# Reordering the hand-over from attention tiles to expert steps: last output product ahead of logits, slots ahead of inner values, GpSimd additions held back

## Chip, cores and metric

One core of one Trainium2 chip. The metric is device microseconds of one execution of the kernel; the median of 3 runs of the kernel before is 1112.19 us (1111.52 to 1112.27).

## What is computed

Input `x` is 4 x 1024 tokens of width 256, all arithmetic in float32. Two layers follow each other, each with a residual:

```
x = x + attention(layernorm(x))     # Nystroem attention, 16 heads, 64 landmarks, 13-tap convolution over tokens, output product with w_fc
x = x + experts(layernorm(x))       # 8 experts, each token goes to 2 of them
```

The attention ends in `out @ w_fc + b_fc`; the kernel adds bias and residual and has the rows `x1` of 128 tokens. The expert layer normalizes `x1`, takes 8 logits per token (`x @ router_w.T`), chooses the two best experts with a jitter threshold and a softmax weight each, and adds for each chosen expert

```
weight * ((silu(x @ w_gate.T) * (x @ w_up.T)) @ w_down.T)
```

## The kernel before, in words

The kernel is written engine by engine, with semaphores between them. There are 36 token steps (`QT`), nine per batch of 1024 tokens; each makes attention scores, exponentials, the weighing by GpSimd, the convolution (`c2_conv`) and, for a tile `m` of 128 tokens, the output product `c2_y(m)`, 16 matmul records into bank 6 of PSUM. Tiles 0 to 31 exist (`MT` is 32). Bank 6 holds one tile at a time, so the next product waits until VectorE has added the residual in `rows_out(m)` (line 1110); TensorE's wait is `bank6_read`.

Tiles are routed in nine groups: seven of four tiles (0 to 6), then group 7 (tiles 28 and 29) and group 8 (tiles 30 and 31). The constants are `LATE` = 6, `NG - 2` = 7, `NG - 1` = 8. The chain for one group is:

- VectorE: `statistics` (lines 1115 and 1116) for each tile, then `inverse_deviations` (1123 to 1131), whose end releases `c2_rs`.
- ScalarE: `norm_rows` (776), one activation for each tile.
- TensorE: `c2_tp`, four transpose records for two tiles (1742). ScalarE: `norm_columns` (783). TensorE: `c2_late_lg`, the logits of two tiles (1758).
- VectorE: `choices` (1146, then 1164 to 1176), whose end releases `d_hot`. TensorE: `c2_counts` (1800). ScalarE: `gap_exponentials` (806).
- VectorE: `slots` (1183 to 1202): weights of the two experts, the counts copied out of PSUM by `take_counts` (1152), places by running sums, and the row indices `idx`, whose end releases `d_meta`.
- GpSimd: `scatter` (587), two indirect DMAs for each tile, which write normalized rows into `xs_d`, sorted by expert.

When group 8 is placed, VectorE counts (`sizes`) and builds tables of work items: `whole_items` (1254 to 1259) and `table` (1263 to 1273). The first table releases `d_units`, on which SyncE loads the sorted rows of the first full items (473), after the scatters have landed.

The expert stage is a chain of 128-token steps `n`, in items `a` of one or two steps. TensorE transposes the rows of an item (`x_columns`, 1846), makes `hidden(0, n)` and `hidden(1, n)` (gate and up products, 1883) and later `down(n)` (1926). ScalarE copies the transposed rows (`rows_transposed`, 813) and takes Silu of the gate product (`gate_out`, 820). VectorE multiplies (`hidden_out`, 1288, which releases `m_hid`) and weighs the result of down (`rows_weighed`, 1300). GpSimd adds the rows to the output (`add_rows`, 608), again an indirect DMA. VectorE also copies each item's gate and up weights (`expert_weights`, 1317). Steps 0 to 4 (items 0 to 2) are "early": their rows belong to an expert chosen after group 4, and were scattered and loaded before. Step 5 is `BLOCK[FIRST]`, the first step of item 3.

Each engine runs its queue in order. What matters around the change is the order written out by hand where the two stages meet. On TensorE, after token step 37:

```
c2_tp(7,0) | late_lg(7,0) x_columns(0) c2_y(31) | hidden(0,0) hidden(1,0) counts(7) c2_tp(8,0)
hidden(0,1) [wait counts of 7 taken] late_lg(8,0) hidden(1,1) down(0) x_columns(1) counts(8) down(1)
hidden(0,2) hidden(1,2) hidden(0,3) x_columns(2) down(2) hidden(1,3) hidden(0,4) down(3) x_columns(3) hidden(1,4) ...
```

The wait in brackets stands because the logits of group 8 and the counts of group 7 lie in the same bank 5. On VectorE the generic `token_step` goes on to step 39: `rows_out(29)` statistics, `inverse_deviations(7)`, `slots(6)`; `rows_out(30)` statistics, `choices(7)`; `rows_out(31)` statistics, `inverse_deviations(8)`; then `hidden_out(0)`, `slots(7)`, `choices(8)`, `hidden_out(1)`, `slots(8)`, `sizes`, `rows_weighed(0)`, the first table, `hidden_out(2)`.

ScalarE has one set of function tables loaded at a time. Exp and Silu are in different sets; the other activations here (Copy, Identity) run under either. The loads are records of their own (ACT_TABLE_LOAD).

## Time and profile before

| | us |
|---|---|
| median of 3 runs | 1112.19 |
| the profiled execution | 1118.69 |
| span in its trace | 1117.0 |
| TensorE busy in the span | 1068.3 |
| VectorE busy | 643.6 |
| ScalarE busy | 319.1 |
| GpSimd busy | 299.3 |

The profiled execution stands 6.50 us above the median. The granted clock of TensorE over its span is 0.995 of full speed. Times in the text are us from the start of the span. The place where the change works lies between 715 and 785 us.

### The profile page before, as it was taken

To read this page: it belongs to the slowest core of one execution; us is meant where nothing else is said; L and a number is where in the kernel's file an instruction comes from. 1 tells how busy PE (TensorE), PEld (TensorE's weight loads), DVE (VectorE), ACT (ScalarE), POOL (GpSimd) and SP (SyncE) were. 2 spreads that over 40 slices of the span, in tenths; PEclk is the share of its full clock that TensorE was granted. 3 is DMA by queue.
4 is the path that set the end of the run, shared out by engine and by line. 5 is a ranking of instruction groups with operands and counts; after the bars stand their busy time and mean duration, and the time that the engine had idled before them with its cause. 6 is when DMAs were issued, how large, how long until landed. Compare 5 with 4: busy or idle time off the path is not lost. (4 is left out here: it accounts for less than half of the span.)

```text
span 1117.0 us, 22941 instructions
## 1 busy us (share of the span) xinstructions
PE 1068.3 (96%) x9126; PEld 857.3 (77%) x9126; DVE 643.6 (58%) x1376; ACT 319.1 (29%) x471; POOL 299.3 (27%) x303
## 2 busy tenths in 40 slices
PE   4999999999989999999999999979999999999996
PEld 4888888888878756666676666768877877878795
DVE  7457755565558576677777778755434434343332
ACT  4433232222324422332332332331122122121210
POOL 6000000000020013225535535551333333423333
PEclk9999999999999999999999999999999999999999
DMA  9300000000300040222411323343423223333122
GB/s 336 125 1 1 1 1 1 1 1 1 97 3 0 2 190 20 105 67 67 144 62 63 104 75 113 109 123 88 87 47 48 47 44 53 49 51 45 20 30 24
DMA packets 48252, 68.27 MB, mean 61 GB/s; under 512 B 8224, under 2 KB 41504, under 8 KB 47136
## 3 DMA queue, kind: packets, MB, share of 16 engines
q1 hardware_dynamic: 34288, 46.83, 13.4%
q0 software_dynamic: 13440, 16.93, 9.1%
q10 hardware_dynamic: 432, 3.24, 0.7%
q8 instruction: 62, 1.02, 0.4%
q14 instruction: 30, 0.25, 0.1%
HBM read 41.43 MB, written 26.59 MB: 61 GB/s over the span
## 5 line engine op out<-in xcount | busy, mean ns | idle before, releaser
L1883 PE MATMUL ps<-mem 128*128 128x256 f32 (+1 forms) x1152 | 221.9, 345 | 0.0
L1883 PEld LDWEIGHTS ps<-mem 128*128 128x128 f32 x1152 | 190.1, 191 | 27.2 <-issue 7.5
L608 POOL DMA_INDIRECT out<-mem x60 | 100.6, 1676 | 196.8 <-DVE mem L1300 151.1
L1288 DVE TENSOR_TENSOR mem<-mem,ps 128x512 f32<-128x512 f32 x66 | 45.3, 687 | 156.8 <-PE ps L1883 131.3
L1729 PE MATMUL ps<-mem 128*128 128x512 f32 x288 | 129.4, 593 | 0.0
L573 POOL TENSOR_TENSOR mem<-mem,small 128x1024 f32<-128x1024 f32 x36 | 68.6, 1906 | 224.8 <-DVE small L1222 120.2
L1926 PE MATMUL ps<-mem 128*128 x480 | 115.3, 384 | 6.6 <-DVE mem L1288 6.6
L820 ACT ACTIVATE mem<-ps 128x512 f32<-128x512 f32 x66 | 39.4, 597 | 285.8 <-PE ps L1883 248.7
L1782 PE MATMUL ps<-mem 128*128 128x256 f32 x512 | 119.4, 387 | 0.0
L1479 PE MATMUL ps<-mem 128*128 128x256 f32 x512 | 117.3, 382 | 0.6 <-ACT mem L694 0.6
L1440 PE MATMUL ps<-mem 128*128 128x256 f32 x512 | 114.5, 380 | 0.0
L1782 PEld LDWEIGHTS ps<-mem 128*128 128x128 f32 x512 | 95.5, 192 | 15.0 <-issue 3.2
L1440 PEld LDWEIGHTS ps<-mem 128*128 128x128 f32 x512 | 95.6, 190 | 12.7 <-issue 0.3
L1479 PEld LDWEIGHTS ps<-mem 128*128 128x128 f32 x512 | 94.8, 190 | 13.5 <-issue 0.8
L1926 PEld LDWEIGHTS ps<-mem 128*128 128x128 f32 x480 | 89.4, 192 | 18.1 <-issue 7.3
L1729 PEld LDWEIGHTS ps<-mem 128*128 128x128 f32 x288 | 54.2, 190 | 54.8 <-issue 52.7
L587 POOL DMA_INDIRECT xs_d<-mem,idx x64 | 62.4, 975 | 56.5 <-DVE idx L1202 40.6
L1774 PEld LDWEIGHTS ps<-mem 128*64 128x64 f32 x1152 | 57.1, 137 | 20.7 <-issue 20.3
L1774 PE MATMUL ps<-mem 128*64 128x116 f32 x1152 | 65.1, 266 | 0.8 <-POOL mem L573 0.8
L795 ACT ACTIVATE mem<-ps 128x928 f32<-128x928 f32 (+2 forms) x36 | 31.6, 877 | 119.8 <-PE ps L1774 89.7
L1317 DVE COPY mem<-mem 128x2048 f32 x51 | 62.1, 1238 | 5.7 <-issue 2.9
L1300 DVE TENSOR_SCALAR mem<-ps,mem 128x256 f32<-128x256 f32 x66 | 29.7, 480 | 48.4 <-PE ps L1926 46.4
(239 smaller groups left out, 1383.7 us busy)
## 6 DMA issues: line engine op xcount, KB each, us to landing
mem<-w_gu SPq DMA_DIRECT2D x9, 1024.0 KB, 5.8
mem<-xs_d SPq DMA_DIRECT2D x22, 260.0 KB, 2.8
mem<-x SPq DMA_DIRECT2D x8, 512.0 KB, 8.8
mem<-x SPq DMA_DIRECT2D x32, 128.0 KB, 2.3
out<-mem SPq DMA_DIRECT2D x32, 128.0 KB, 1.7
mem<-w_down SPq DMA_DIRECT2D x8, 512.0 KB
xnt_d<-mem ACTq DMA_DIRECT2D x3, 1056.0 KB, 5.6
mem<-xnt_d SPq DMA_DIRECT2D x3, 1056.0 KB, 4.8
```

Of the source, the lines that this page charges most:

```text
L573: pool.tensor_tensor(a1[:, u], ex[:, u].rearrange("p (h c) -> p h c", h=H), ri[:, 16 * u:16 * u + 16].unsqueeze(2).to_broadcast([P, H, M]) ...
L587: pool.indirect_dma_start(out=xs_d, out_offset=bass.IndirectOffsetOnAxis(ap=idx[:, u, v, c:c + 1].bitcast(U32), axis=0), in_=xd[:, u, v, c ...
L608: pool.indirect_dma_start(out=out_rows, out_offset=bass.IndirectOffsetOnAxis(ap=rows_to.bitcast(U32), axis=0), in_=ys[:, r % YRING], in_of ...
L1288: dve.tensor_tensor(hid[:, n % 2], sil[:, n % 2], bank(2 + n % 2), ALU.mult).then_inc(s("m_hid"), 1)
L1317: dve.tensor_copy(v, w_gu_s[:, e]).then_inc(s("m_w"), 1)
L1440: mm = pe.matmul(bank(t // 2)[:, t % 2 * 2 * P:(t % 2 + 1) * 2 * P], xnts[b][:, k, HALO + P * t:HALO + P * t + P], g3c[:, b, k, j * P:(j + ...
L1479: mm = pe.matmul(bank(6)[:, k * 2 * P:(k + 1) * 2 * P], xna[:, b, t, k * P:(k + 1) * P], e3s[m % 4][:, t], start=(t == 0), stop=(t == RT - 1))
L1729: mm = pe.matmul(bank(2 * u + half), xnt2[b % 2][:, k, TO * t:TO * t + P], g1c[:, b, k, 512 * half:512 * half + 512], start=(k == 0), stop ...
L1774: mm = pe.matmul(bank(4, 2)[c:c + 64, (h // 2) * P:(h // 2) * P + TO], a1[:, q % 2, h], band[:, h], start=True, stop=True)
L1782: mm = pe.matmul(bank(6)[:, 0:D], cvt[:, j, at_:at_ + P], pm[:, b, j], start=(j == 0), stop=(j == J - 1))
L1883: mm = pe.matmul(bank(2 * c + n % 2)[:, i * size:(i + 1) * size], w[:, k, c, f * P:(f + 1) * P], xst[:, a % 2, k, 0:size], start=(k == 0), ...
L1926: mm = pe.matmul(bank(down_bank(a, b))[:, 0:D], hid[:, u, i * size + b * P:i * size + (b + 1) * P], w_d_s[:, e, f], start=(f == 0), stop=( ...
```

## The change

It leaves every computation as it is and changes the order of instructions on four engines, with one added wait.

```
@@ gpsimd
             for u in range(X1):
                 pool.wait_ge(s(f"x1_out{u}"), 16 * (MT // X1))
+            pool.wait_ge(s("m_hid"), 3)
             for r in range(EBLK):
                 wait_alone(pool, "m_y", r + 1)
                 add_rows(r, xs_e[:, r, D + 1:D + 2])
@@ scalar
             norm_columns(NG - 2, 0)
             rows_transposed(0)
-            gap_exponentials(NG - 2)
-            gate_out(0)
             norm_rows(NG - 1, 0)
             norm_rows(NG - 1, 1)
+            gate_out(0)
             norm_columns(NG - 1, 0)
+            gap_exponentials(NG - 2)
             gate_out(1)
             gap_exponentials(NG - 1)
@@ vector: slots(g) is now slot_weights(g), up to take_counts(g), and slot_places(g), the rest
-            for i in range(QT + 4):
+            for i in range(QT + 1):
                 token_step(i)
+            rows_out(MT - 3)
+            statistics(MT - 3, NG - 2)
+            inverse_deviations(NG - 2)
+            slot_weights(LATE)
+            rows_out(MT - 2)
+            slot_places(LATE)
+            statistics(MT - 2, NG - 1)
+            rows_out(MT - 1)
+            statistics(MT - 1, NG - 1)
+            inverse_deviations(NG - 1)
+            choices(NG - 2)
             dve.wait_ge(s("c2_a1"), QT)
+            slots(NG - 2)
             hidden_out(0)
-            slots(NG - 2)
             choices(NG - 1)
             hidden_out(1)
             slots(NG - 1)
             sizes()
             rows_weighed(0)
             whole_items(0, 8)
+            hidden_out(2)
             table(2 * P, u_eid, u_row, "d_units")
-            hidden_out(2)
@@
                     table(P, t_eid, t_row, "d_rest")
-                if n == BLOCK[FIRST] + 1:
+                if n == BLOCK[FIRST] + 2:
                     taken(NT, P)
                     whole_items(C - 1, 5)
                     table(C, c_eid, c_row, "d_rest")
@@ tensor
             c2_tp(NG - 2, 0)
             pe.wait_ge(s("c2_cvt"), cvt_count(QT - 1))
+            bank6_read(last)
+            c2_y(MT - 1)
             c2_late_lg(NG - 2, 0)
             x_columns(0)
-            bank6_read(last)
-            c2_y(MT - 1)
             pe.wait_ge(s("e_w_in"), 16)
             pe.wait_ge(s("c2_sub"), QT)
             hidden(0, 0)
             hidden(1, 0)
-            c2_counts(NG - 2)
             c2_tp(NG - 1, 0)
             pe.wait_ge(s("d_taken"), NG - 2)
             hidden(0, 1)
+            c2_counts(NG - 2)
             pe.wait_ge(s("d_taken"), NG - 1)
             c2_late_lg(NG - 1, 0)
             hidden(1, 1)
```

## Rows read from the trace of the kernel before

**Rows 1.** Page, busy us of each engine, share of the span, instructions.

```profile
PE 1068.3 (96%) x9126; PEld 857.3 (77%) x9126; DVE 643.6 (58%) x1376; ACT 319.1 (29%) x471; POOL 299.3 (27%) x303
```

**Rows 2.** Timeline of TensorE: start, us, engine, line, operation, count, [idle before it <-releaser].

```profile
720.48 0.66 PE L1742 MATMUL ps<-ids,mem 128*128 128x128 f32 x4 [0.42 <-ACT mem L776]
721.91 1.24 PE L1758 MATMUL ps<-rw,mem 128*128 128x8 f32 x8 [0.78 <-ACT mem L783]
...
723.89 4.67 PE L1782 MATMUL ps<-mem 128*128 128x256 f32 x16
728.39 3.62 PE L1883 MATMUL ps<-mem 128*128 128x256 f32 x16
...
733.93 0.66 PE L1742 MATMUL ps<-ids,mem 128*128 128x128 f32 x4 [1.57 <-ACT mem L776]
...
743.38 5.34 PE L1883 MATMUL ps<-mem 128*128 128x256 f32 x24
748.56 0.38 PE L1846 MATMUL ps<-ids,mem 128*128 128x128 f32 x2
753.76 3.44 PE L1926 MATMUL ps<-mem 128*128 x8 [4.82 <-DVE mem L1288]
...
783.68 1.99 PE L1926 MATMUL ps<-mem 128*128 x8 [0.88 <-DVE mem L1288]
```

**Rows 3.** Busy time by stretch: length, PE, PEld, DVE, ACT, POOL, PEclk, DMA share, GB/s.

```profile
719.20:722.60 3.40, 2.20 (x15) 1.54 (x14) 3.02 (x19) 1.82 (x3) 0.00 (x0) 1.00 0.00 0
722.60:726.00 3.40, 3.40 (x13) 2.98 (x13) 2.78 (x16) 0.60 (x1) 2.56 (x3) 0.50 0.33 116
...
732.80:736.20 3.40, 2.27 (x12) 1.83 (x12) 1.62 (x8) 1.67 (x3) 0.00 (x0) 1.00 0.74 296
```

**Rows 4.** Timeline of ScalarE, same columns.

```profile
732.36 1.52 ACT L776 ACTIVATE mem<-mem,small 128x512 f32<-128x512 f32 x2 [0.33 <-issue]
...
736.97 1.28 ACT L806 ACT_TABLE_LOAD   x1
740.41 0.23 ACT L806 ACTIVATE mem<-mem 128x32 f32<-128x32 f32 x1 [2.16 <-DVE mem L1176]
...
748.50 0.60 ACT L820 ACTIVATE mem<-ps 128x512 f32<-128x512 f32 x1 [5.20 <-remote]
```

**Rows 5.** Timeline of GpSimd, same columns.

```profile
751.11 1.58 POOL L608 DMA_INDIRECT out<-mem  x1 [0.30 <-issue]
```

**Rows 6.** Timeline of VectorE, same columns.

```profile
719.96 0.22 DVE L1152 COPY mem<-ps 128x64 f32<-128x64 f32 x1
...
722.01 0.43 DVE L1110 TENSOR_TENSOR mem<-ps,mem 128x256 f32<-128x256 f32 x1
...
728.59 0.42 DVE L1110 TENSOR_TENSOR mem<-ps,mem 128x256 f32<-128x256 f32 x1 [2.47 <-PE ps L1782]
...
732.16 0.16 DVE L1131 SCALAR_TENSOR_TENSOR small<-small 128x2 f32<-128x2 f32 x1
...
735.04 0.18 DVE L1183 TENSOR_TENSOR mem<-mem 128x32 f32<-128x32 f32 x1
...
737.30 0.17 DVE L1202 CAST idx<-mem 128x4 int32<-128x4 f32 x1
...
740.20 0.17 DVE L1176 TENSOR_TENSOR mem<-mem 128x16 f32<-128x16 f32 x1
...
752.91 0.69 DVE L1288 TENSOR_TENSOR mem<-mem,ps 128x512 f32<-128x512 f32 x1 [2.65 <-remote]
...
776.16 0.16 DVE L1278 TENSOR_SCALAR small<-small 128x8 f32<-128x8 f32 x1
...
780.18 0.24 DVE L1273 TENSOR_SCALAR tab<-tab,small 128x24 int32<-128x24 f32 x1
```

**Rows 7.** Timeline of SyncE's DMA issues, same columns.

```profile
751.31 3.83 SPq L473 DMA_DIRECT2D mem<-xs_d  x4
```

**Rows 8.** Page, DMA issues: count, KB each, median us from issue to landing.

```profile
mem<-xs_d SPq DMA_DIRECT2D x22, 260.0 KB, 2.8
```

More of the change, by code:

```diff
@@ L614, in _ @@
                 pool.wait_ge(s(f"x1_out{u}"), 16 * (MT // X1))
+            pool.wait_ge(s("m_hid"), 3)
             for r in range(EBLK):
@@ L855, in _ @@
             rows_transposed(0)
-            gap_exponentials(NG - 2)
-            gate_out(0)
             norm_rows(NG - 1, 0)
             norm_rows(NG - 1, 1)
+            gate_out(0)
             norm_columns(NG - 1, 0)
+            gap_exponentials(NG - 2)
             gate_out(1)
@@ L1178, in slots, with slot_weights @@
             def slots(g):
+                slot_weights(g)
+                slot_places(g)
+            def slot_weights(g):
                 (m, n), (u, v0) = GROUPS[g], HOME[g]
@@ L1195, in slots, with slot_places @@
                     take_counts(g)
+            def slot_places(g):
+                n, (u, v0) = GROUPS[g][1], HOME[g]
+                t = both[:, :, 0:n]
                 dve.wait_ge(s("d_taken"), g + 1)
@@ L1342, in token_step @@
                     choices(g)
-            for i in range(QT + 4):
+            for i in range(QT + 1):
                 token_step(i)
+            rows_out(MT - 3)
+            statistics(MT - 3, NG - 2)
+            inverse_deviations(NG - 2)
+            slot_weights(LATE)
+            rows_out(MT - 2)
+            slot_places(LATE)
+            statistics(MT - 2, NG - 1)
+            rows_out(MT - 1)
+            statistics(MT - 1, NG - 1)
+            inverse_deviations(NG - 1)
+            choices(NG - 2)
             dve.wait_ge(s("c2_a1"), QT)
+            slots(NG - 2)
             hidden_out(0)
-            slots(NG - 2)
             choices(NG - 1)
@@ L1354, in _ @@
             whole_items(0, 8)
+            hidden_out(2)
             table(2 * P, u_eid, u_row, "d_units")
-            hidden_out(2)
             dve.wait_ge(s("wgu_in"), 16 * E)
@@ L1375, in _ @@
                     table(P, t_eid, t_row, "d_rest")
-                if n == BLOCK[FIRST] + 1:
+                if n == BLOCK[FIRST] + 2:
                     taken(NT, P)
@@ L1934, in _ @@
             pe.wait_ge(s("c2_cvt"), cvt_count(QT - 1))
+            bank6_read(last)
+            c2_y(MT - 1)
             c2_late_lg(NG - 2, 0)
             x_columns(0)
-            bank6_read(last)
-            c2_y(MT - 1)
             pe.wait_ge(s("e_w_in"), 16)
@@ L1942, in _ @@
             hidden(1, 0)
-            c2_counts(NG - 2)
             c2_tp(NG - 1, 0)
@@ L1946, in _ @@
             hidden(0, 1)
+            c2_counts(NG - 2)
             pe.wait_ge(s("d_taken"), NG - 1)
```

## The prediction

> **What bounds the kernel now.** I read the page first: TensorE is busy 96% of the span and no other engine passes 58% [rows 1]. So an edit is worth what it takes out of TensorE's queue, idle time or time at the lower clock, and only where nothing behind it takes it back. TensorE's timeline between the stages comes next [rows 2]. It has four waits: 0.42 us, 0.78 us, 1.57 us and 4.82 us. Two groups of products ran at half pace as well. The output product of tile 31 took 4.67 us where the 16 records of the same shape behind it took 3.62, and `down(2)` took 3.44 us for 8 records where 1.73 is usual (8 x 0.216: 24 such records start and pass in the 5.18 us from 743.38 to 748.56). The busy time by stretch shows why: from 722.6 the granted clock is 0.50, that is 1.2 GHz in place of 2.4, and ahead of that TensorE had waits, transposes and products of 8 columns; in 732.8 to 736.2, behind 1.57 us of idle, it stayed at 1.00 [rows 3]. Then comes the full expert stage, with one wait of 0.88 us at 783.68 [rows 2].
>
> The long wait deserves a second look. `down(2)` waits for `hidden_out(2)` at 752.91, and that engine's own wait, 2.65 us, has the releaser "remote", no instruction of this trace [rows 6]. The same holds for ScalarE at 748.50: it reads the first of three products that TensorE issued from 743.38, done by 0.216 x 8 at about 745.1, and starts 3.4 us after that [rows 2, 4]. VectorE and ScalarE get on some 0.2 us after GpSimd's second addition ends at 752.69 [rows 5, 6]. So TensorE's signals came late here, for a reason that the trace doesn't name. The wait and the lower clock behind it cost 4.82 + 1.71 = 6.53 us. The profiled execution, 1118.69, stands 6.50 us over the median of 1112.19. I take it from this that the ordinary runs lack this stall. Without it VectorE would be at 743.8 behind its count of rows (740.4 + 0.6 for `hidden_out(1)` + 2.4 for the slots + 0.4), weigh two blocks in 0.9 and make the first table in 3.6 (the third took 4.26 with 0.7 of `taken` ahead, 776.16 to 780.42 [rows 6]): 748.3. `hidden_out(2)` would end at 749.0, as TensorE gets to `down(2)` at 748.95.
>
> **The change, part by part.** I follow the new order in the profiled execution's time.
>
> Bank 6. VectorE now has `rows_out(30)` ahead of the places of group 6. The weights with the counts' copy end at 720.18 [rows 6], so it runs at 720.2 in place of 722.01 and ends at 720.63. TensorE's transposes of group 7 stay at 720.48 and take 0.44 us to the next start; `c2_y(31)` then starts at 720.9, in place of 723.89, and needs 3.45 us to the next start at full clock: 724.4. The wait of 0.78 us vanishes, since the copy that it was for now runs beside the product. The logits of group 7 take 0.9 and `x_columns(0)` 0.44: 725.75. Here a new wait appears. ScalarE's copy of these columns (0.60, as the activation of the same size [rows 4]) was hidden by `c2_y(31)` and now isn't: hidden(0,0) starts at 726.6, idle 0.85 us. Both hidden products end at 730.05, where before they did at 731.85 (728.39 + 3.45) [rows 2]. That is 1.8 us gained, 1.05 of it the lower clock.
>
> Group 8's normalization. `rows_out(31)` is ready at 724.6. From 728.59 to the end of the deviations at 732.32 was 3.73 us [rows 6]: 728.35 now. `norm_rows` stands ahead of `gate_out(0)`, takes 1.52 [rows 4], ends at 729.9, and TensorE is busy to 730.05. So the 1.57 us wait is gone. Transposes 0.45 and hidden(0,1) 1.73 end at 732.2, counts(7) at 732.55; `choices(7)` (2.9 us, from 737.47 to 740.37 in group 8 [rows 6]) had ended near 731.0.
>
> The wait ahead of group 8's logits. It is for `take_counts(7)`, now behind `choices(7)` and behind the exponentials of group 7, and VectorE waits for these. On ScalarE these stood ahead of `gate_out(0)`, under the same tables as the exponentials before. Now they stand between two Silus, so there are two loads of tables more. ScalarE: load 729.9 to 731.2, Silu to 731.8, `norm_columns` to 732.4, load to 733.7, exponentials (0.23) to 733.9. Slot weights take 1.26 us to the end of the counts' copy (their share of 2.4): 735.2. TensorE stands idle from 732.55 to 735.2, 2.65 us, with `hidden_out(0)`, `choices(8)` and all of VectorE's queue behind the same wait. A load costs 1.28 us by its own record [rows 4]. What it holds up can't be less; the nearest activation behind one starts 3.44 us after the load's start (736.97 to 740.41), but that one waited for VectorE [rows 4]. I take 1.28, and keep 3.44 as the upper end.
>
> The Trainium skill, page "ScalarE: Activation LUTs", section "What ACT_TABLE_LOAD costs", puts a switch of tables at about 2.66 us, the load of 1283 ns and a drain of 1380 ns. The load agrees with the trace; the drain no row shows. By that price the wait of TensorE would be 2.8 us longer.
>
> On to `down(2)`. Logits of group 8 0.9 and hidden(1,1) 1.75 end at 737.85. Before it was 739.04 (733.93 + 0.49 + 1.90 + 0.91 + 1.81). **Lead 1.2 us.** Then down(0), x_columns(1), counts(8), down(1) as before: `hidden_out(0)` comes at 737.0, the choices of group 8 end at 739.8, `hidden_out(1)` at 740.4, when TensorE gets there, and the third load of tables lies beside `down(0)`. The three hidden products and x_columns(2) end at 747.55. `slots(8)` runs 740.4 to 742.8 (2.4, from 735.04 to 737.47 [rows 6]), sizes and weighing to 744.1, item counts (1.3 of the 3.6) to 745.4, `hidden_out(2)` with the up product at 745.8, done at 746.5, since it is ahead of the table (2.3 us). So `down(2)` doesn't wait.
>
> GpSimd. Its second addition starts at 751.11, the first 1.9 us ahead of it (1.58 and 0.30 of issue [rows 5]), right behind the scatters. These move by the 0.5 us of group 8's indices, so they last to about 748.7, after `m_hid` has reached 3. The added wait costs nothing; the cover is the scatter, and if `hidden_out(2)` were late the additions would move by as much, ahead of buffers that are free for 8 rows. The scatter of group 6 moves 0.45 us later, behind it nothing waits.
>
> The first table ends at 748.7. Group 8's indices come at 742.8, before at 743.3; its scatters and SyncE's row loads, which wait for their landing, move by the same 0.5 us: 750.8 for 751.31, landed 2.8 us later at 753.6 [rows 7, 8]. `x_columns(3)` comes at 754.5. It holds by 0.9 us: this is what is late next.
>
> The third table moves from step 6 to step 7. It ended at 780.42 and pushed a weight copy, a weighing and `hidden_out(7)` behind it, for which TensorE stood 0.88 us [rows 2, 6]. Now `hidden_out(7)` comes first, and the 4.2 us of table lie before the next product is done. **Gain 0.9 us.** SyncE gets the entry for the quarter items some 5 us later, and the first of them is wanted 20 us later.
>
> Sum: 1.2 + 0.9 = 2.1 us against ordinary runs, 1112.19 - 2.1 = 1110.1. Against the profiled execution 6.5 + 2.1 = 8.6: 1118.69 - 8.6 = 1110.1, provided that its own signals come in time.
>
> **The rivals.** *The lower clock moves on.* TensorE has 3.9 us with little but a wait and narrow products (732.2 to 736.1). The stretch of 719.2 to 722.6 led to a fall, the one with 1.57 us idle didn't [rows 3], and this lies between them and longer. A fall like that of 753.76 costs 1.7 us: 1111.8. *The loads of tables cost more* (slower). If each of the two on the path costs 2.66 us, within the 3.44 bound, that is 2.76 us more, the wait is 5.4 us, like the 4.82 us behind which the clock fell: 1110.1 + 2.8 + 1.7 = 1114.6. With the fall, the change loses time from 0.2 us more for each load, and by over 0.2% from 1.3. For it speaks that no row shows an activation right behind a load; against it that the loads themselves start without a gap. *The stall is in ordinary runs too.* Then the gain is 6.5 + 1.2 + 0.9 = 8.6, 1103.6, or 2 us less if the signal for `hidden_out(2)`, sent at 745.8, still comes 3.4 us late like the one at 748.50: 1105.6. Against it stands the match of 6.53 and 6.50. *The lead is given back*, at the landing of rows or at a signal that comes late before 735: no change, 1112.2.
>
> **How the numbers follow.** Forecast 0.40 (own range 1109 to 1111), clock 0.20, loads 0.13, stall 0.17, given back 0.10. A measurement tells 0.2%, 2.2 us, from no change, so the forecast lies on that bound and I put 0.22 of its 0.40 on the faster side: with 0.17 of the stall and 0.03 of the clock case, 0.42. Slower is the loads' case with a little of the others: 0.15. Same 0.43. The range takes in the clock case and the near end of the stall and goes up to most of the loads': 1105.2 to 1113.8.
>
> **What would show it.** In the changed profile: `c2_y(31)` near 720.9 in 3.7 us; a wait of about 2.7 us before the second L1758 group, released by VectorE's L1152; five ACT_TABLE_LOADs between 726 and 745 for three; no wait at `down(2)`; none near 775 to 785. A span near 1108.4, where the clock stays whole. I am wrong if that wait is over 4 us, if the clock drops behind it, or if the time falls by more than 5 us, which would put the stall into the ordinary runs.

## The result, and the profile after

| | before | after |
|---|---|---|
| median, 14 runs each, taken beside each other | 1112.01 us | 1114.07 us |
| lowest to highest | 1110.94 to 1113.80 | 1112.63 to 1115.68 |
| profiled execution | 1118.69 | 1115.68 |
| its span | 1117.0 | 1114.0 |

The ratio is 1.0017, interval 1.001 to 1.0024: some 2 us slower, where 2.1 us faster was forecast, and outside the range. The profiled execution before, with its long stall, lies outside the 14 timed runs, so the two profiles stand the other way round than the medians do. Each is compared with the prediction's sum, not with the other.

TensorE after, same columns as [rows 2]. L1801 is now `c2_y`, L1761 `c2_tp`, L1777 the late logits, L1902 `hidden`, L1945 `down`.

```profile
719.79 0.66 PE L1761 MATMUL ps<-ids,mem 128*128 128x128 f32 x4 [0.43 <-ACT mem L777]
720.28 3.62 PE L1801 MATMUL ps<-mem 128*128 128x256 f32 x16
...
725.96 3.69 PE L1902 MATMUL ps<-mem 128*128 128x256 f32 x16 [0.78 <-ACT mem L814]
729.49 0.60 PE L1761 MATMUL ps<-ids,mem 128*128 128x128 f32 x4
...
737.25 1.88 PE L1777 MATMUL ps<-rw,mem 128*128 128x8 f32 x8 [5.08 <-DVE mem L1153]
738.98 3.76 PE L1902 MATMUL ps<-mem 128*128 128x256 f32 x8
742.53 2.97 PE L1945 MATMUL ps<-mem 128*128 x8
...
753.35 1.89 PE L1945 MATMUL ps<-mem 128*128 x8
```

Up to 732 it goes as predicted. The output product runs right behind the transposes at full clock (3.62 us for the 4.67 of [rows 2]), the new wait for the copied columns is 0.78 us (forecast 0.85), and group 8's transposes wait no more (1.57 before). Then comes a wait of 5.08 us where 2.65 was forecast, and behind it the logits and hidden(1,1) take twice their time, and `down(0)` takes 2.97 us where the next ones take 1.97. `down(2)` at 753.35 has no wait; before, it had 4.82 us.

Busy time by stretch of after, same columns as [rows 3]: the granted clock falls from 1.00 to 0.50, which is 1.2 GHz for 2.4, behind a stretch in which TensorE has no instruction at all.

```profile
732.80:736.20 3.40, 0.00 (x0) 0.00 (x0) 0.19 (x1) 2.42 (x4) 0.00 (x0) 0.75 0.11 39
736.20:739.60 3.40, 2.35 (x10) 2.26 (x11) 2.89 (x17) 2.85 (x3) 0.38 (x1) 0.50 0.00 0
```

ScalarE after, as [rows 4]. L784 is `norm_columns`, L807 the exponentials, L821 Silu.

```profile
729.04 1.28 ACT L821 ACT_TABLE_LOAD   x1
730.33 0.60 ACT L821 ACTIVATE mem<-ps 128x512 f32<-128x512 f32 x1
733.74 0.60 ACT L784 ACTIVATE mem<-ps 128x512 f32<-128x512 f32 x1 [2.81 <-remote]
734.35 1.28 ACT L807 ACT_TABLE_LOAD   x1
735.64 0.23 ACT L807 ACTIVATE mem<-mem 128x32 f32<-128x32 f32 x1
735.89 1.28 ACT L821 ACT_TABLE_LOAD   x1
737.18 0.60 ACT L821 ACTIVATE mem<-ps 128x512 f32<-128x512 f32 x1
```

Here is the difference. The transposes were issued from 729.49, and hidden(0,1) behind them starts at 729.93, so the columns of group 8 stand in PSUM near 730.1. ScalarE is free at 730.93. It copies them at 733.74, and the releaser is "remote": the signal is late. The load of tables, the exponentials, VectorE's slot weights (first at 735.97) and the copy of the counts stand behind. The loads themselves cost what was forecast: 734.35 plus 1.28 is 735.63, and the activation starts at 735.64.

GpSimd after, as [rows 5]: the first and the eighth of group 6's scatters, and the first addition.

```profile
722.36 1.01 POOL L587 DMA_INDIRECT xs_d<-mem,idx  x1 [9.25 <-DVE idx L1210]
...
731.25 0.96 POOL L587 DMA_INDIRECT xs_d<-mem,idx  x1 [0.30 <-issue]
...
753.61 1.62 POOL L608 DMA_INDIRECT out<-mem  x1 [0.30 <-issue]
```

The addition follows group 8's scatters after 0.30 us of issue, so the added wait on `m_hid` costs nothing. The eighth scatter ends at 732.21, and the late copy starts 1.53 us after it. The experiments turn on that distance.

VectorE after, as [rows 6]: `hidden_out(2)` waits 1.38 us for the up product that it multiplies, and TensorE gets to `down(2)` behind it.

```profile
751.77 0.69 DVE L1296 TENSOR_TENSOR mem<-mem,ps 128x512 f32<-128x512 f32 x1 [1.38 <-PE ps L1902]
```

The chain of all of TensorE's waits from 715 to the end, after (waiting line, releaser: us in total, times, longest). The wait near 783 of [rows 2] is gone; the 0.9 left stands at the end of the kernel.

```profile
PE ps L1777 <- DVE mem L1153: 5.1, 1, 5.1
PE ps L1945 <- DVE mem L1296: 0.9, 1, 0.9
PE ps L1819 <- DVE mem L1111: 0.8, 1, 0.8
PE ps L1902 <- ACT mem L814: 0.8, 1, 0.8
PE ps L1761 <- ACT mem L777: 0.4, 1, 0.4
```

### The profile page after: what moved, and what is told of

The parts are those of the page before. It is cut to its first block, busy times and chain, and to the rows that moved or that the text cites. A ratio compares the mean times of both kernels' runs of the same rounds, so it can differ in the third digit from the quotient of the medians.

```text
span 1114.0 us, 22943 instructions
## 1 busy us (share of the span) xinstructions
PE 1067.5 (96%) x9126; PEld 857.1 (77%) x9126; DVE 642.8 (58%) x1376; ACT 321.5 (29%) x473; POOL 300.1 (27%) x303
## 3 DMA queue, kind: packets, MB, share of 16 engines
q10 hardware_dynamic: 432, 3.24, 0.7%
## 4 chain that ended last, share of the span: by engine, by line
PE 83%; DVE 6%; issue 4%; POOL 3%; DMA 2%; ACT 2%; another core or an unknown queue 0%; POOLq 0%; DVEq 0%; ACTq 0%
PE ps L1902 17%; PE ps L1498 10%; PE ps L1459 9%; PE ps L1801 9%; PE ps L1945 9%; PE ps L1748 8%; PE ps L1793 5%; PE ps L1886 2%; DMA out<-mem 2%; PE ps L1615 1%; PE ps L1865 1%; PE ps L1433 1%; PE ps L1634 1%; PE ps L1939 1%; PE ps L1513 1%
## 5 line engine op out<-in xcount | busy, mean ns | idle before, releaser
L1902 PE MATMUL ps<-mem 128*128 128x256 f32 (+1 forms) x1152 | 223.7, 347 | 0.8 <-ACT mem L814 0.8
L1902 PEld LDWEIGHTS ps<-mem 128*128 128x128 f32 x1152 | 191.1, 192 | 28.6 <-issue 8.5
L1801 PE MATMUL ps<-mem 128*128 128x256 f32 x512 | 118.4, 384 | 0.0
L821 ACT ACTIVATE mem<-ps 128x512 f32<-128x512 f32 x66 | 39.4, 597 | 273.3 <-PE ps L1902 245.2
L1945 PE MATMUL ps<-mem 128*128 x480 | 114.7, 382 | 0.9 <-DVE mem L1296 0.9
L1801 PEld LDWEIGHTS ps<-mem 128*128 128x128 f32 x512 | 94.7, 190 | 14.7 <-issue 3.2
L1945 PEld LDWEIGHTS ps<-mem 128*128 128x128 f32 x480 | 89.2, 192 | 12.0 <-issue 1.1
```

Of the source, the lines that this page charges most:

```text
L1801: mm = pe.matmul(bank(6)[:, 0:D], cvt[:, j, at_:at_ + P], pm[:, b, j], start=(j == 0), stop=(j == J - 1))
L1902: mm = pe.matmul(bank(2 * c + n % 2)[:, i * size:(i + 1) * size], w[:, k, c, f * P:(f + 1) * P], xst[:, a % 2, k, 0:size], start=(k == 0), ...
L1945: mm = pe.matmul(bank(down_bank(a, b))[:, 0:D], hid[:, u, i * size + b * P:i * size + (b + 1) * P], w_d_s[:, e, f], start=(f == 0), stop=( ...
```

## The experiments

The kernels were timed in five groups, each on one chip beside runs of the kernel before, and every ratio is to those. "Below" and "above" compare medians; a ratio with its interval is worked out from the single runs, so it can differ a little from the ratio of the medians. The chips differ, as it turned out, and this is part of the answer.

### First chip: parts of the change, and the kernel before (1109.79 us, 27 runs)

**before_again**, the kernel before, one execution with its profile.

> The kernel before, profiled once more, to see whether the 4.82 us wait at the down product of step 2 (753.76 in the first profile) belongs to the kernel or to that one execution. Theory S (the stall belongs to single executions): the wait is under 1 us here, the down product runs at full clock, and the profiled time is within 2 us of the median of 1112.0. Rival (it is in every execution): a wait of 4 to 5 us again, and the profiled time as near to the median as it can be with that wait in both.

Measured 1109.04 us, span 1107.3. The stall of the first profile is absent; `down(2)` starts without a wait:

```profile
745.63 1.99 PE L1926 MATMUL ps<-mem 128*128 x8
```

So the 6.5 us of stall are no fixed part of the kernel, as assumed. But 1109 is also 3 us below the median of 1112: "without the stall" and "an ordinary run on the first chip" are not the same thing.

**exp_first**: the exponentials of group 7 ahead of both Silus, so two loads of tables fewer.

```
             norm_rows(NG - 1, 1)
+            gap_exponentials(NG - 2)
             gate_out(0)
             norm_columns(NG - 1, 0)
-            gap_exponentials(NG - 2)
             gate_out(1)
```

> The changed kernel, with the exponentials of group 7 on ScalarE put ahead of the Silu of step 0, so that the two additional loads of tables are gone; all else as changed. Theory L (the loads and the Silu, the copy of columns and their signal in front of the exponentials make TensorE wait 5.08 us ahead of the logits of group 8, and the clock falls behind it): that wait is under 1.5 us, the clock stays whole there, and the time is 3.5 to 5.5 us under the changed kernel, 1108.6 to 1110.6, ratio to before 0.997 to 0.9985. Rival E (the late wait for the exponentials is not what costs in ordinary runs; the earlier output product or the held back additions do): within 1 us of the changed kernel, ratio 1.001 to 1.0025.

Measured 1107.85, ratio 0.9982 (0.9973 to 0.9991). TensorE's timeline:

```profile
733.51 1.03 PE L1777 MATMUL ps<-rw,mem 128*128 128x8 f32 x8 [0.88 <-ACT mem L784]
734.39 3.48 PE L1902 MATMUL ps<-mem 128*128 128x256 f32 x8
```

The wait is 0.88 us and its releaser the copy of columns. The clock fell behind it all the same. The copy of columns (L784) starts at 732.77, as ScalarE comes free. That is 0.07 us behind GpSimd's eighth scatter, so this row alone can't tell whether the signal was in time; the other rows of this chip show that it was ("What the runs say together"). The kernel after wasn't run here, so what the exponentials' place is worth by itself is open.

**table3_later**: the kernel before with only the third table moved.

```
-                if n == BLOCK[FIRST] + 1:
+                if n == BLOCK[FIRST] + 2:
```

> The kernel before with only the third table moved from step 6 to step 7. Theory (the prediction's term): the wait of 0.88 us at the down product of step 7 goes, nothing comes back, 0.9 us faster, ratio 0.9992. Rival: the later row loads of the quarter items or the delayed table make TensorE wait elsewhere, ratio 1.000 or above.

Measured 1108.65, ratio 0.9992 (0.9981 to 1.0002). In the chain of waits `down` waits once for 0.9 us, where before_again has 1.8 in two:

```profile
PE ps L1926 <- DVE mem L1288: 0.9, 1, 0.9
```

**tail_only**: this and the two other late parts, without the new order at the front.

```
+            pool.wait_ge(s("m_hid"), 3)
...
+            hidden_out(2)
             table(2 * P, u_eid, u_row, "d_units")
-            hidden_out(2)
```

> The kernel before with the three parts of the change that lie behind the hand-over: the GpSimd additions behind m_hid 3, the inner values of step 2 ahead of the first table, the third table one step later. Theory L: none of these loses time, ratio 0.997 to 0.9995 (0.9 us for the third table, and up to 2 us more if the inner values of step 2 were late in ordinary runs too). Rival G (one of these three is what made the change slower): ratio 1.001 or more.

Measured 1109.14, ratio 0.9984 (0.9975 to 0.9993), so the tail is a gain of 0.8 to 2.8 us on this chip by the interval, 0.65 by the medians, though its one profile had the lower clock in the output product of tile 31, as [rows 2] has.

### Second chip: the wait ahead of group 8's logits (before 1118.10 us, 33 runs)

**after_again**, the kernel after.

> The changed kernel once more, beside the others on the same chip. Its first profile had a wait of 5.08 us ahead of the logits of group 8, of which 2.81 us was ScalarE waiting for a late signal of the transposes ahead. Theory L (the two loads lie on the path in every execution, the late signal only in some): the wait is 2.4 to 3.2 us, the clock falls or stays, ratio to before 1.0005 to 1.002. Rival D (the late signal is all of it): the wait is 2.3 us too, but the time is under before, ratio 0.998 to 0.9995, as the prediction had it.

Measured 1115.27, ratio 0.9982 (0.9967 to 0.9997). The same change that loses 2 us in the first measurement gains 2 to 3 here, because the kernel before takes 1118.1 (1112.68 to 1119.96), close to the 1118.69 of its profile with the stall. These 33 times fall into two groups with nothing between them: nine from 1112.68 to 1114.83 (middle 1113.81) and 24 from 1117.07 to 1119.96 (middle 1118.4). Against the lower group the kernel after is 1.5 us slower here too. The wait is there as in after: 5.30 us, with ScalarE idle for 3.02 us ahead of the copy of columns, releaser "remote".

**silu0_copy**: it leaves out the Silu of step 0 and copies the gate product instead.

```
-                act.activation(sil[:, n % 2], bank(n % 2), ACT.Silu)
+                act.activation(sil[:, n % 2], bank(n % 2), ACT.Copy if n == 0 else ACT.Silu)
```

> The changed kernel with the Silu of step 0 replaced by a plain copy, so that step 0 takes the gate product without its Silu; the order stays, the exponentials of group 7 stay behind it, but the two loads of tables ahead of them are gone. Theory L (loads): the wait ahead of the logits of group 8 falls by 2.5 us to under 0.7 us, and the time falls by 2.5 to 4.5 us under the changed kernel. Rival O (the late place of the exponentials behind the Silu and the copy of columns costs, not the loads): the wait stays over 2 us.

Measured 1113.50, ratio 0.9966 (0.9951 to 0.9981). ScalarE and TensorE:

```profile
733.54 0.60 ACT L784 ACTIVATE mem<-ps 128x512 f32<-128x512 f32 x1 [4.41 <-remote]
734.03 0.22 ACT L807 ACTIVATE mem<-mem 128x32 f32<-128x32 f32 x1
```

```profile
735.63 1.88 PE L1777 MATMUL ps<-rw,mem 128*128 128x8 f32 x8 [3.83 <-DVE mem L1153]
```

Two loads fewer took 1.5 us off the wait (5.30 to 3.83), one load and not two. ScalarE's own wait shows why: it grew from 3.02 to 4.41. The first load lay beside the late signal and was free; only the second stood behind it. And 3.83 us remain with neither load, so the loads are not the cause of what the forecast missed.

**exp_columns_first**: exponentials and columns ahead of both Silus.

```
             norm_rows(NG - 1, 1)
-            gate_out(0)
-            norm_columns(NG - 1, 0)
             gap_exponentials(NG - 2)
+            norm_columns(NG - 1, 0)
+            gate_out(0)
             gate_out(1)
```

> The changed kernel with the exponentials of group 7 and then the copy of group 8's columns ahead of the Silu of step 0. With the exponentials alone moved, TensorE waited 0.88 us for that copy, which stood behind a load and a Silu. Theory L: the wait is 0.2 to 0.5 us, ratio to before 0.997 to 0.9985, by up to 1 us better than with the exponentials alone. Rival: the Silu of step 0 is now late for the inner values, TensorE waits at the first down product, ratio 0.9985 or above.

Measured 1111.49, ratio 0.9947 (0.9928 to 0.9965), 3.8 us below the kernel after.

```profile
736.49 0.60 ACT L784 ACTIVATE mem<-ps 128x512 f32<-128x512 f32 x1 [3.47 <-remote]
```

The signal is as late as ever, but nothing is left behind it: TensorE waits 2.55 us, for the copy itself. This profile is of the slowest of its ten executions (1115.45); the second and third profile of this order, at 1110.82 and 1111.28, show the same wait as 2.30 and 2.42.

**front_only**: the kernel after without its three late parts.

> The changed kernel without its three later parts: no wait of GpSimd for m_hid, inner values of step 2 behind the first table, third table at step 6. Theory L (the hand-over's own order loses what the later parts win): 1 to 1.6 us slower than the changed kernel beside it, ratio to before 1.001 to 1.003. Rival G: the same as the changed kernel within 0.5 us.

Measured 1116.13, ratio 0.9997 (0.9981 to 1.0012), 0.86 us above the kernel after. In the chain of waits the wait near 783 is back:

```profile
PE ps L1944 <- DVE mem L1295: 1.8, 2, 0.9
```

### Third chip: what makes the signal late (before 1113.22 us, 27 runs)

**after_third**, the kernel after.

> The changed kernel as the reference of this group. Two chips differed: on one the kernel before ran in 1109.8 us and no signal of TensorE was late in five profiles of four kernels, on the other it ran in 1118.1 and signals were late by 2 to 6 us while the last weight load and GpSimd's scatters ran. Theory (late signals are a matter of the chip, and the change trades one place of harm for another): where the profile shows no late signal at the copy of columns of group 8, the wait ahead of its logits is 2.3 to 2.9 us and the ratio to before 0.998 to 1.0005; where it shows one, the wait is about 5.2 us, and the ratio is set by whether the kernel before has its own stall at the down product of step 2 in most of its runs (0.997 to 0.999) or not (1.001 to 1.003).

Measured 1114.85, ratio 1.0017 (1.0008 to 1.0026), the wait 5.12 us, ScalarE idle for 2.83 us ahead of the copy. (The expectation speaks of five profiles on the first chip; there are four, of four kernels.)

**load_late**: the last load of expert weights, which lands in this stretch, is held back.

```
                         sp.wait_ge(s("c2_y"), m + 1)
+                        if m == MT - 1:
+                            sp.wait_ge(s("m_hid"), 2)
```

> The changed kernel, with the last 1 MB load of gate and up weights (issued at 724.8) held back on SyncE until the inner values of step 1 are made, near 743. It is wanted near 755. Theory W (this load is what makes TensorE's signals late at 729 to 734): no wait of ScalarE with the releaser remote at the copy of columns, the wait ahead of the logits falls from about 5.2 to about 2.5 us, the time falls by 2 to 4 us. Rival S (GpSimd's scatters do it): the signal is as late as in the reference.

Measured 1115.01, ratio 1.0015 (1.0006 to 1.0024). The load is issued at 743.59 and the signal is late as before:

```profile
733.71 0.60 ACT L786 ACTIVATE mem<-ps 128x512 f32<-128x512 f32 x1 [2.81 <-remote]
```

This theory fell.

**scatter_late**: all eight scatters of group 6 wait until group 8's columns are copied.

```
                         if sent_at(g, h) == i and 2 * h < GROUPS[g][1]:
+                            if g == LATE and h == 0:
+                                pool.wait_ge(s("c2_x1t"), PAIRS[NG])
                             scatter(g, 2 * h)
```

> The changed kernel, with the eight scatters of group 6 (from 722.4) held back on GpSimd until the columns of group 8 are copied, near 731 to 734. Rival S (GpSimd's scatters make TensorE's signals late): no remote wait at the copy of columns, the wait falls to about 2.5 us. Theory W (the weight load does): the signal stays late, the wait stays over 4 us. If either alone removes it, both together are needed for the lateness.

Measured 1117.96, ratio 1.0047 (1.0033 to 1.006), 3 us worse than after. At the old place all is in time:

```profile
733.76 1.16 PE L1779 MATMUL ps<-rw,mem 128*128 128x8 f32 x8 [2.17 <-DVE mem L1155]
```

That is the forecast's wait of 2.65 us, with both loads on its path. The clock fell behind it all the same: hidden(1,1), next in line, takes 3.55 us where 1.97 is usual. But group 6's and 7's scatters are now one run of twelve, ending at 746.71, and the next signal is late by far more (ScalarE):

```profile
747.37 0.60 ACT L816 ACTIVATE mem<-ps 128x512 f32<-128x512 f32 x1 [8.75 <-remote]
```

**exp_columns_second**, the order of exp_columns_first on this chip.

> The changed kernel with the exponentials of group 7 and the copy of group 8's columns ahead of the Silu of step 0, a second time. Theory L: 3 to 4.5 us under the changed kernel on this chip too (1111.5 against 1115.3 the first time). Rival: under 1 us, the first difference was one of that chip.

Measured 1111.52, ratio 0.9986 (0.9977 to 0.9995), 3.3 us below after_third.

### Fourth chip: cutting the run of scatters (before 1112.36 us, 27 runs)

**after_fourth**, the kernel after.

> The kernel after, for comparison on this chip. If the run of scatters holds TensorE's signals: the copy of group 8's columns starts 1.5 to 1.8 us after the eighth scatter of group 6 ends, the wait ahead of the logits is 5.1 to 5.3 us. If this is a chip without late signals: the copy starts behind the Silu without a releaser 'remote', the wait is near 2.2 to 2.7 us, and the time is 1 us or more below the kernel before.

Measured 1114.19, ratio 1.0015 (1.0006 to 1.0024); GpSimd's eighth scatter, and ScalarE's copy 1.49 us after its end:

```profile
731.03 0.96 POOL L587 DMA_INDIRECT xs_d<-mem,idx  x1 [0.30 <-issue]
```

```profile
733.48 0.60 ACT L784 ACTIVATE mem<-ps 128x512 f32<-128x512 f32 x1 [2.78 <-remote]
```

**scatter_split**: as scatter_late, with `h == 1` for `h == 0`, so that four go at once and four wait.

> The last four of group 6's eight scatters wait until group 8's columns are copied, so that the first run of four ends near 727.3. Theory (a run of scatters holds the signals until it has ended): the columns are copied near 730.3 with no releaser 'remote', the wait ahead of the logits is 2.2 to 2.7 us, and the copy does not follow the fourth scatter by 1.5 us. The four moved ones run from 731 to 736, and signals sent in them may be late, the next in need being those for down(0) and the logits of group 8. If nothing else is late, 3 to 4 us below after_fourth; if the lateness moves on, as with scatter_late, between 2 below and 1 above. Rival (the lateness belongs to the place or to a transfer there, not to the scatters): the copy of columns still starts near 733.7 and the wait is still 5.1, time as after_fourth. On a chip without late signals both are equal within 0.1%.

Measured 1111.73, ratio 0.9993 (0.9984 to 1.0002), 2.5 us below after_fourth. The copy of columns starts at 731.36 behind the Silu, the wait is 2.17 us, and the clock is still whole for the logits (1.06 us for the 1.88 of after), but not for hidden(1,1) behind them:

```profile
734.87 1.06 PE L1779 MATMUL ps<-rw,mem 128*128 128x8 f32 x8 [2.17 <-DVE mem L1155]
735.78 3.45 PE L1904 MATMUL ps<-mem 128*128 128x256 f32 x8
```

The four held scatters and group 7's four follow each other now, a new run of eight that ends at 742.69, and 1.60 us after that:

```profile
741.73 0.96 POOL L587 DMA_INDIRECT xs_d<-mem,idx  x1 [0.30 <-issue]
```

```profile
744.29 0.60 ACT L816 ACTIVATE mem<-ps 128x512 f32<-128x512 f32 x1 [4.60 <-remote]
```

**exp_columns_split**: the same split on top of exp_columns_first.

> As scatter_split, with the exponentials of group 7 and the copy of group 8's columns ahead of both Silus. Theory: no late signal at the copy of columns, so no wait over 1 us ahead of the logits, where the same order without the split showed 2.3 to 2.6 us; 4 to 6 us below after_fourth, if nothing behind is late. Rival (place or transfer): the wait stays 2.3 to 2.6 us and the time 3.3 to 3.8 us below after_fourth.

Measured 1111.52, ratio 0.9994 (0.9985 to 1.0004), 2.7 us below after_fourth and under the 4 expected. The wait ahead of the logits is 0.28 us, and behind it the clock stays whole (hidden(1,1) 1.97 us). The run of eight behind it ends at 741.22, the signal comes at 742.81, and the three hidden products wait for it:

```profile
743.46 7.11 PE L1904 MATMUL ps<-mem 128*128 128x256 f32 x24 [3.94 <-ACT mem L816]
```

### Fifth chip: pauses between the runs (before 1117.51 us, 29 runs)

**exp_columns_third**, the order of exp_columns_first.

> The exponentials and columns ahead of the Silus, group 6's eight scatters in one run, for comparison on this chip. On a chip with late signals: copy of group 8's columns 1.5 to 1.8 us after the eighth scatter, wait 2.3 to 2.6 us ahead of the logits.

Measured 1111.14, ratio 0.9952 (0.9937 to 0.9968), the wait 2.42 us.

**two_pauses** and **three_pauses**: on top of it, group 7's scatters wait for group 8's counts, and in the second kernel group 8's for the third Silu.

```
+                            if g == LATE and h == 1:
+                                pool.wait_ge(s("c2_x1t"), PAIRS[NG])
+                            if g == NG - 2:
+                                pool.wait_ge(s("d_taken"), NG)
+                            if g == NG - 1:                  # three_pauses alone
+                                pool.wait_ge(s("m_sil"), 3)
```

> As exp_columns_third, with group 6's last four scatters held until group 8's columns are copied, and group 7's four until the counts of group 8 are taken; group 7's and group 8's follow each other, a run of eight from about 739. Theory (the length of a run decides): no copy with releaser 'remote' before 740, wait ahead of the logits under 0.5 us, VectorE's copy of the counts of group 8 near 737.5 instead of 742.9; a late signal 1.5 us after the end of the last run, near 750, which may hold hidden_out(2) and down(2): between 2 and 5 us below exp_columns_third where this costs nothing, equal where it costs 3. Rival (each scatter behind the first four delays signals, pause or not): a 'remote' copy between 733 and 740, and no gain on exp_columns_third.

> As two_pauses, with group 8's four scatters held as well, until the gate product of step 2 is through Silu, so that all of the runs have four. Theory: no releaser 'remote' on ScalarE or VectorE between 725 and 752, the wait at down(2) under 0.5 us, 3 to 6 us below exp_columns_third, or less where group 8's rows then land too late for x_columns(3). Rival: a 'remote' copy remains and the time is that of exp_columns_third or above.

Measured 1113.82 and 1114.08, ratios 0.9976 (0.9959 to 0.9993) and 0.9983 (0.9967 to 1.0): both 2.7 to 2.9 us worse than the order without pauses. The first half is as the theory has it: no late signal before 740, a wait of 0.28 us. But with the indices of group 8 ready earlier, its four scatters and the two additions join group 7's, ten in one run. VectorE's `hidden_out(3)` and TensorE's `down(3)` in two_pauses:

```profile
755.29 0.69 DVE L1300 TENSOR_TENSOR mem<-mem,ps 128x512 f32<-128x512 f32 x1 [5.26 <-remote]
```

```profile
756.13 3.51 PE L1949 MATMUL ps<-mem 128*128 x8 [4.30 <-DVE mem L1300]
```

That is the stall of the kernel before, one step later: 5.26 for its 2.65 at VectorE, 4.30 for 4.82 at TensorE, the lower clock behind it [rows 2, 6]. `down(2)` itself, at 746.37, had no wait. The third pause did nothing: the Silu it waits for had ended at 742.32 and group 7's scatters lasted to 744.4. So a run of four was not tried there.

### What the runs say together

The last scatter or addition of a run, and the first late start on another engine behind its end:

| kernel | length of the run | ends | late start | distance |
|---|---|---|---|---|
| after | 8 | 732.21 | 733.74 | 1.53 |
| after_again | 8 | 732.53 | 734.26 | 1.73 |
| after_fourth | 8 | 731.99 | 733.48 | 1.49 |
| exp_columns_first | 8 | 734.72 | 736.49 | 1.77 |
| scatter_split | 8, later | 742.69 | 744.29 | 1.60 |
| exp_columns_split | 8, later | 741.22 | 742.81 | 1.59 |
| scatter_late | 12 | 746.71 | 747.37 | 0.66 |
| before, group 6 | 8 | 732.70 | 734.44 | 1.74 |
| before [rows 5, 6] | 4, a gap of 1.09, 6 | 752.69 | 752.91 | 0.22 |
| two_pauses | 10 | 755.22 | 755.29 | 0.07 |
| three_pauses | 10 | 754.04 | 754.11 | 0.07 |

The lateness follows the scatters, not a place in the program: moving the run moves it. The profiles not in the table (silu0_copy, front_only, after_third, load_late, exp_columns_second and exp_columns_third) have the same run of eight and distances of 1.51 to 1.72. The distance is no rule, though. The table takes starts behind the end of a run, and there are late ones inside runs as well: 745.60 and 748.50 in the kernel before, 749.35 in two_pauses, 748.20 and 749.65 in three_pauses.

Nor does the length of a run decide. In the attention stage GpSimd issues four scatters at a time, and ScalarE's copy of the convolution's product starts late behind them; in the kernel before, the fourth ended at 709.83 and the product was made at 709.1:

```profile
710.91 0.94 ACT L795 ACTIVATE mem<-ps 128x928 f32<-128x928 f32 x1 [3.72 <-remote]
```

In after, the copy at 596.77 comes 3.0 us after its product and 0.86 us after a run of four. TensorE doesn't wait for these. Other runs of four to six held nothing up, as the one of six from 748.54 in after, so what makes one run harmful and another not is open.

On the first chip none of this is seen. Its four profiles have no start with the releaser "remote" on ScalarE or VectorE in the whole trace; each of the other sixteen, the two first profiles included, has at least three ahead of 713 alone. The load on the DMA engines doesn't make the difference here: from 730 to 732 they are as busy in before_again (1.04, 411 GB/s) as in after from 728 to 730 (1.00, 390). In table3_later the run of eight ends at 731.99, and the copy of group 8's columns starts at 731.97, 0.75 us behind the start of the transposes that release it:

```profile
731.97 0.60 ACT L783 ACTIVATE mem<-ps 128x512 f32<-128x512 f32 x1 [0.75 <-PE ps L1742]
```

What sits between the scatters and a signal of TensorE, whether GpSimd's issuing or the transfers that it issues, and why one chip lacks it, stays open.

The clock is a second thing. In every profile of the new order with a wait of 0.88 us or more ahead of group 8's logits it fell to 0.50 at the logits or right behind them, with the signal in time (scatter_late, scatter_split) or not. Only with the wait at 0.28 us did it hold. From group 8's transposes to `down(0)` the forecast has 7.80 us and after 13.04; with the signal in time it is 9.26 in scatter_late and 9.00 in scatter_split. So the late signal costs about 4 us of the difference, and the clock 1.2 to 1.5 us net even without it.

## Why the prediction was wrong

**The step that failed** is the term "2.65 us, idle from 732.55 to 735.2", together with the sentence that the sum holds "provided that its own signals come in time". They don't. And the sum's other condition, "where the clock stays whole", fails by itself: behind a wait of 2.17 us with the signal in time, shorter than the forecast one, hidden(1,1) still took 3.24 and 3.39 us to the next start for 1.75 (scatter_split, scatter_late). Set against the profile, the sum closes. The wait began at 732.17, 0.38 earlier than forecast (this execution was 0.69 us ahead at the transposes of group 7 already), and took 2.43 us more than 2.65. The clock fell behind it, so that the logits took 1.73 us to the next start for 0.9, and hidden(1,1) 3.55 for 1.75: 2.63 more. `down(0)` begins at 742.53 instead of 737.85, 4.68 late. From there to `down(2)` it is 10.82 us for 9.91 in [rows 2], 0.91 more, by `down(0)` at the lower clock. Together 5.59 us (against the sum; the text's own place for `down(2)`, 747.55, is 0.2 us earlier than its sum has it), and the span of 1114.0 is 5.6 above the forecast's 1108.4. Nothing outside this stretch is missing. The medians differ by less, 1114.07 - 1110.1 = 3.97; the profiled execution is the slowest of the 14, and how the others saved 1.6 us wasn't seen. after_again and after_fourth, with 2.16 and 2.41 us for `down(0)` in place of 2.97, point to the clock.

The mechanism stood in the text with a wrong price. It was found in [rows 4, 6] as "TensorE's signals came late here", and carried as one clause of the last rival, "a signal that comes late before 735", with no change as its worst. It was taken as an accident of one execution at one place, where it belongs to a kind of work, GpSimd's scatters, and eight of them stand beside this very step in every execution. The rows to see it were at hand: seen beside GpSimd's timeline, the two late starts of [rows 4, 6] stand in and right behind one run of scatters and additions. The 0.2 us between GpSimd's last addition and VectorE's start was noted and not followed up. And behind the run of eight itself the trace of before has a late start, `hidden_out(0)`, 1.74 us after the eighth scatter:

```profile
734.44 0.69 DVE L1288 TENSOR_TENSOR mem<-mem,ps 128x512 f32<-128x512 f32 x1 [2.12 <-remote]
```

`slots(7)` stands behind it, so group 7's scatters start at 738.28 and end 1.09 us ahead of group 8's; in before_again `hidden_out(0)` starts at 729.38 and that gap is 2.77 us. So the long stall of the kernel before may follow from this earlier late signal. No run tests that.

**Other steps.** Bank 6 and the earlier output product: right, to 0.2 us in each part. The GpSimd wait that costs nothing: right. `down(2)` without a wait: right, and as forecast VectorE is there before the up product (751.77). What the forecast left out is that the signals must come in time there too. They did; group 7's and 8's scatters stand 4.57 us apart, where before they had 1.09. That the gap did it is argued from two_pauses, which closed it and brought a stall back. The third table, forecast 0.9: its wait is gone in both orders, and the runs give 1.1 us (table3_later, by the medians; its interval just takes in no change) and, for the tail as a whole, 0.86 (front_only against after) and 0.65 (tail_only).

**The rivals.** *Loads that cost 2.66 each* was the slower one, and its time, 1114.6, is near the result, by luck: its mechanism is refuted. Three activations start 1.29 us after their load started. The page "ScalarE: Activation LUTs" of the Trainium skill, section "What ACT_TABLE_LOAD costs", adds a drain of 1380 ns to a load; no record here shows it. silu0_copy took two loads away and 3.83 us of wait were left. *The lower clock moves on*: it did, in all of the profiles of after, and in exp_first behind only 0.88 us of idle. This rival was right in its mechanism: its 1.7 us is near the 1.5 to 1.6 that hidden(1,1) lost with the signal in time, and half of the 3.5 us that the clock cost behind the late one. *The stall is in ordinary runs too*: in part, and by chip. The kernel before took 1112.0 in the first measurement and 1109.8, 1112.4, 1113.2, 1117.5 and 1118.1 on the five chips. The kernel after took 1114.1, and 1114.2, 1114.9 and 1115.3 on three of these. So after is much the same wherever it ran, and the sign of the change lies in how many runs of before have the stall: 1.0017, 1.0017 and 1.0015 against 0.9982. On the second chip it is 24 of 33 by the two groups of times, on the fifth 19 of 29 (1116.96 to 1119.65, and ten from 1112.83 to 1114.91), in the first measurement none of 14. That the upper group is the stall is inferred from the 1118.69 of its profile; no profile was taken on these chips. The match of 6.53 and 6.50 compared a profiled execution with a median that probably came from different chips (1118.69 is inside the range of the second chip's runs of before and outside that of the first measurement), so it was no proof of what an ordinary run lacks. The kernel before has no profile on the chips with times in between, so what lies between its 1109.8 and its 1112 to 1113 is open, as is the time of after on the chip where signals are in time; it wasn't run there.

**A version that beats both** is exp_columns_first. It took 1111.1 to 1111.5 us on three chips, ratios 0.9947, 0.9952 and 0.9986, always below before and, on two of them, 3.3 and 3.8 us below after. Against the lower groups of before on the second and fifth chip it is 2.2 to 2.3 us faster. It leaves the late signal and moves what stood behind it.

## What to carry to other kernels

Read the single times before trusting a median: two groups in it mean that two things are being compared. When a wait in the profile has the releaser "remote", lay the timelines of all engines beside it, GpSimd's DMA queue first, and ask where else in the program the same company is kept, before calling it an accident. Put as little as possible behind a signal that may be late: with the exponentials and the columns ahead of the Silus the same lateness cost 3 to 4 us less. And a lead won upstream can close the gap between two bursts and bring a stall of its own, so an earlier start has to be followed through every queue, not only through the engine that bounds the kernel.

## What the runs showed of the hardware

- In the first profiles and on four of the five chips of the experiments, signals of TensorE to ScalarE and VectorE came some 2 to 7 us late around runs of indirect DMAs from GpSimd (1.27 us from one scatter to the next): 1.5 to 1.8 us after the end of a run of eight, 0.07 to 0.7 after one of ten or twelve, some inside such runs, and 1.1 us after a run of four (710.91 in before). Other runs of four to six held nothing up. On the first of the five they weren't late anywhere.
- The granted clock fell to 0.50 behind 5.1 us of idle, behind 2.17 in scatter_split, and in exp_first behind 0.88; in the first profile it held behind 1.57 [rows 3]. In before_again the output product of tile 31 ran at full clock, in the first profile and in tail_only at half, with the same instructions ahead. A fall is not to be read from the program alone.
- A load of tables is 1.28 us, the activation behind it starts 0.01 us later, and it is free when it lies beside a wait.
- One profiled execution can stand 6.5 us from the median, and the medians of one kernel 8 us apart between chips. The times of one kernel on one chip can fall into two groups 4.6 us apart.
